# Encoder attention: statistics, a division of sums and scalings of a norm placed over three rounds of the second sequence of a pair instead of two

## The reference, cut to what matters

```python
q = (h @ wq + bq_); k = (h @ wk + bk_); v = (h @ wv + bv_)      # split into heads
scores = jnp.einsum('bhqd,bhkd->bhqk', q, k) * scale
scores = scores * smask
a = jax.nn.softmax(scores, axis=-1)
att = jnp.einsum('bhqk,bhkd->bhqd', a, v)
att = att.transpose(0, 2, 1, 3).reshape(Bx, Sx, Dx) @ wo + bo_
h = _ln(h + att, g1, be1)
ff = jax.nn.gelu(h @ w1 + b1_, approximate=False) @ w2 + b2_
h = _ln(h + ff, g2, be2)
```

## Time and profile before

| | |
|---|---|
| median of 3 runs | 4765.77 us (4759.86 to 4777.94) |
| the profiled execution | 4746.57 us, span 4744.7 us |
| PE busy | 3758.3 us, 79% of the span |
| PEld busy | 2577.3 us, 54% |
| DVE busy | 2783.0 us, 59% |
| ACT busy | 1913.5 us, 40% |
| POOL busy | 778.8 us, 16% |
| largest group of instructions | DVE, reductions L748: x1152, 749.8 us |

### The profile page before, as it was taken

The page is one execution under the profiler, slowest core; times in us unless marked ns, Lnnn a source line. Parts: engine busy times, 40 slices in busy tenths (PEclk is TensorE's granted clock), DMA queues, the critical chain, the costliest instruction groups (busy, mean ns, idle before and its releaser), DMA issues. The chain is left out here.

```text
span 4744.7 us, 71737 instructions
## 1 busy us (share of the span) xinstructions
PE 3758.3 (79%) x27543; PEld 2577.3 (54%) x27543; DVE 2783.0 (59%) x6776; ACT 1913.5 (40%) x2979; POOL 778.8 (16%) x1058
## 2 busy tenths in 40 slices
PE   5998998998989989969999644577745465997996
PEld 3666666666666667647777311255423332443664
DVE  5756747747747657552222477888679865112673
ACT  2554554545645545533333333322212112332443
POOL 2222222222222122130000000000000032002221
PEclk8999999999999999989999766599857666998997
DMA  5414424424325234200000000000000000001440
GB/s 135 114 38 110 113 52 98 100 51 116 80 64 118 63 83 114 63 35 6 1 1 1 14 0 0 0 1 1 1 5 0 4 0 25 0 0 47 99 98 24
DMA packets 156736, 222.56 MB, mean 47 GB/s; under 512 B 16158, under 2 KB 136350, under 8 KB 139422
## 3 DMA queue, kind: packets, MB, share of 16 engines
q10 hardware_dynamic: 19656, 107.37, 10.3%
q1 hardware_dynamic: 136750, 110.69, 8.6%
HBM read 154.42 MB, written 60.82 MB: 45 GB/s over the span
## 5 line engine op out<-in xcount | busy, mean ns | idle before, releaser
L748 DVE TENSOR_REDUCE enc_mx<-psum 128x2 f32<-128x512 f32 (+1 forms) x1152 | 749.8, 685 | 296.0 <-PE psum L457 292.6
L889 ACT ACTIVATE enc_e<-psum 128x1024 f32<-128x1024 f32 (+1 forms) x768 | 580.9, 808 | 423.5 <-PE psum L476 367.6
L457 PE MATMUL psum<-enc_ks,enc_qs 80*128 80x128 bf16 (+1 forms) x3072 | 459.4, 255 | 124.9 <-DVE enc_mx L748 108.9
L476 PE MATMUL psum<-enc_qs,enc_ks 83*128 83x256 bf16 (+1 forms) x3072 | 383.9, 250 | 20.4 <-DMA enc_qs<-enc_turned_max 15.5
L457 PEld LDWEIGHTS psum<-enc_ks,enc_qs 80*128 80x128 bf16 x3072 | 220.3, 100 | 264.8 <-DVE enc_mx L748 174.7
L487 PE MATMUL psum<-enc_e,enc_v 128*32 128x256 f32 (+1 forms) x6144 | 336.7, 338 | 0.0
L476 PEld LDWEIGHTS psum<-enc_qs,enc_ks 83*128 83x128 bf16 x3072 | 261.9, 99 | 58.2 <-DMA enc_qs<-enc_turned_max 20.1
L1764 ACT ACTIVATE moe_act_h<-psum 128x512 f32<-128x512 f32 x288 | 169.3, 598 | 306.0 <-PE psum L1638 305.8
L1660 PEld LDWEIGHTS psum<-par_s,moe_act_h 128*128 128x128 f32 x2304 | 269.7, 192 | 30.1 <-issue 28.5
L1727 DVE SCALAR_TENSOR_TENSOR moe_acc<-psum,moe_gates,moe_acc 128x128 f32<-128x128 f32 x256 | 72.1, 344 | 345.3 <-PE psum L1660 345.3
L1660 PE MATMUL psum<-par_s,moe_act_h 128*128 128x128 f32 x2304 | 272.6, 275 | 0.0
(11 more groups left out here) (457 smaller groups left out, 7380.3 us busy)
## 6 DMA issues: line engine op xcount, KB each, us to landing
enc_qs<-q_pieces ACTq DMA_DIRECT2D x234, 192.0 KB
enc_ks<-k_pieces ACTq DMA_DIRECT2D x234, 192.0 KB
k_pieces<-enc_pieces SPq DMA_DIRECT2D x240, 128.0 KB, 2.0
q_pieces<-enc_pieces SPq DMA_DIRECT2D x144, 128.0 KB, 2.0
enc_qs<-q_pieces SPq DMA_DIRECT2D x54, 192.0 KB
enc_ks<-k_pieces SPq DMA_DIRECT2D x54, 192.0 KB
rope_qs<-q_pieces ACTq DMA_DIRECT2D x39, 192.0 KB
rope_ks<-k_pieces ACTq DMA_DIRECT2D x39, 192.0 KB
```

What stands on the lines that cost most here:

```text
L457: last = T_.matmul(p1[f % 2][:, i * kw:(i + 1) * kw], qs[0:KEYED, slot, h, j * P:(j + 1) * P], ks[0:KEYED, slot, h, 0:kw], start=True, sto ...
L476: last = T_.matmul(p2[ch][:, g], ks[0:SCORED, slot, 4 * T + g, ch * P:(ch + 1) * P], qs[0:SCORED, slot, 4 * T + g, 0:n], start=True, stop= ...
L748: V.tensor_reduce(mx[:, u % 2, j * HEADS + h0:j * HEADS + h0 + n], p1[f % 2].rearrange("p (h k) -> p h k", h=n), AX_X, ALU.max)\
L889: A.activation(e_of(T, ch), p2[ch], ACT.Exp, scale=HD ** -0.5).then_inc(s_e, 1)
```

## The change

`Chain.statistics` is split in two: `gather` (the four `bn_stats`) and `combine` (the rest). In the attention loop of DVE the second sequence of a pair is ordered anew. `gather` stays in round 1. `combine` goes into round 2, between its first and second reduction. `normalise(layer, u - 1, 1)` goes from the end of round 1 into round 2, between its second and third reduction. The two halves of `apply` go from round 2 to the same places of round 3. In the first sequence of a pair, `normalise(layer, u - 1, 1)` stays where it was. No instruction is added or taken away, and no other engine's stream is touched.

```diff
     def statistics(self, dve, n):
+        self.gather(dve, n)
+        self.combine(dve, n)
+
+    def gather(self, dve, n):
         V = self.c.nc.vector
         dve.wait_ge(self.s_moved, n + 1)
         for t in range(TILES):
             last = V.bn_stats(self.stats[:, t, :], self.rows[:, t, :])
         last.then_inc(self.s_stats, 1)
+
+    def combine(self, dve, n):
+        V = self.c.nc.vector
         dve.wait_ge(self.s_stats, n + 1)
         V.memset(self.c.scratch[:], 0.0)
         for t in range(TILES):
...
                         red(0)
                         if T == 2 and odd and m:
+                            N1.combine(dve, at(layer, GROUPS, m - 1))
+                        if T == 3 and odd and m:
                             N1.apply(dve, at(layer, GROUPS, m - 1), (0, 1))
                         red(1)
-                        if T == 2 and odd and m:
+                        if T == 2 and odd:
+                            normalise(layer, u - 1, 1)
+                        if T == 3 and odd and m:
                             N1.apply(dve, at(layer, GROUPS, m - 1), (2, 3))
...
                         if T == 1 and odd and m:
-                            N1.statistics(dve, at(layer, GROUPS, m - 1))
-                        if T == 1 and u:
+                            N1.gather(dve, at(layer, GROUPS, m - 1))
+                        if T == 1 and u and not odd:
                             normalise(layer, u - 1, 1)
```

## The result

The changed kernel takes 4699.16 us, the median of 4 runs (4693.41 to 4704.41), beside 4770.71 us for the kernel before (4759.86 to 4777.94). The ratio is 0.9862, with a 95% interval of 0.9839 to 0.9885: 66 us less, between 55 and 77; the two medians by themselves lie 72 us apart. The forecast was faster, by 42 us. The rest of this document is about why the walk along DVE's work was right to a few hundredths of a microsecond, while the total was too small and the cause given for the falls of the clock was wrong.

A forecast was written before the change was run, and what follows sets the result against it. DVE was taken to set the pace in round 2 of full odd sequences, PE in the other rounds. A shorter DVE chain (21.6 us) plus the clock (20 us) gave 41.6 us: 4705 against the profile, 4724 against the median; range 4700 to 4754.

The forecast's parts named there:

- The walk through one odd sequence: Rounds 2 and 3 of full odd sequences: DVE's new order, timed with old distances, makes each sequence 0.60 us shorter.
- fill 10: PE's fill in round 2 behind the moved normalisation: it comes at 888.12, with a new wait of 0.8 us.
- The term of 0.60 us: Gain per full odd sequence from DVE's shorter chain up to the last scaling: 36 x 0.60 = 21.6 us.
- What is moved or passed at no cost: POOL's inverse root, bank reuse, exponentials, DMA and sequences 1 and 15: the reordering loses nothing there.
- The slow rival of blocked scalings: Round 3: GpSimd blocks the moved scalings, the last comes 2.7 us later, 76 us slower, 4842; chance 0.02.
- I take all of it: Slow clock in 12 of 36 third rounds, 1.66 us each: all 20 us counted as gain, bounds 0 to 20.
- the single wait of 1.18 us: PE's wait for a reduction in round 2 of odd sequences, taken to precede the clock's falls; it goes.
- The clock falls as often: Third rounds of odd sequences: waits shrink but as many are slow, 26 us gained, 4740; chance 0.15.
- no gain: DVE's chain to the last scaling: new handoffs eat the 0.60 us, leaving noise and some clock, 4760; chance 0.11.
- More than that: DVE's later work starts without pause and new waits overlap: 55 us gained with the clock, 4711; chance 0.06.
- the 69.8: PE's three waits for DVE, 1.94 us per odd sequence, over 36: 69.8 us, upper bound of the waits term.
- The spreading slow clock: Round 3 of odd sequences: later waits cause falls costing 2.6 us each, 52 us slower if all 36, 4818; chance 0.06.

The follow-up runs named there:

- e5: The changed kernel with four more `bn_stats`, into a tile nothing reads, ahead of `gather` in round 1 of odd sequences: 4759.17 us, ratio to the kernel before 0.9976.
- e6: The changed kernel with `gather` moved to round 0 of the odd sequence and `combine` to round 1: 4677.86 us, ratio to the kernel before 0.9803.
- e9: The changed kernel with `gather` and `combine` together again in round 1: a single run, 4715.42 us, beside 4763.15 us for the kernel before.
- e3: The kernel before, unedited, profiled again for its granted clock: 4772.29 us.
- e4: The kernel before, unedited, profiled once more after e3: 4770.91 us.
- e8: The changed kernel, unedited, run again on the chip of e5 to e7: 4708.77 us, ratio to the kernel before 0.9862.
- e1: The kernel before with only the scalings moved from round 2 to round 3 of odd sequences: 4713.13 us, ratio 0.9907.
- e2: The kernel before with only the normalisation moved from the end of round 1 to behind round 2's second reduction in odd sequences: 4825.03 us, ratio 1.0125.
- e7: As e6, with the normalisation back in round 1 and scalings split between rounds 2 and 3: 4650.66 us, ratio to the kernel before 0.9739.

## Why the prediction was right, and where it was off

- **The walk through one odd sequence** was right step by step. Forecast on the old scale: fill 10 at 888.12, the norm turned at 890.44. Measured, with 17.06 added: 888.08 and 890.40. Rounds 2.33 and 4.85, forecast "about 2.4" and "about 4.8". The term of 0.60 us measured 0.62, 22.3 us for the 36. e5, e6 and e9 change the chain by +0.78, -1.3 and +0.12 us and land within 0.06 us of the same walk.
- **What is moved or passed at no cost** held: POOL's root lies between 869.03 and 870.05, the scalings come at 871.48. Sequence 1 costs next to nothing: in layer 0 fill 10 waits 0.25 us, and PE's wait for the DMA at the start of sequence 2 falls from 0.63 to 0.32 us. The slow rival of blocked scalings falls: the four take 0.60 and 0.59 in pairs, as before. By the rule of the Trainium skill (SBUF — State Buffer, SBUF: two separate sides) they could only have been blocked beside a working GpSimd. In the third round POOL has only its root (1.02 us in the window that starts at 868.95), over before the scalings: the trace is in line with the rule, but no run here tests it.
- **The clock was the term that was mis-sized.** "I take all of it", 20 us, was read from one execution in which 12 of 36 third rounds were slow. That part did come out: 42.5 us in rounds 2 and 3 of the profiled pair (300.6 to 258.1), forecast 41.6. But two more executions had 20 and 22 slow rounds. Against the mean of the two profiles of the changed kernel, e3 and e4 lose 56 us in rounds 2 and 3 (313.2 and 316.4 to 258.3), 22 by the chain and 34 by the clock. A step was missing besides: the falls reach into the next even sequence's first round, which gave 5 us in the profiled pair and 8 in e3 and e4. By these two profiles the clock was worth 42 us and not 20, together 64 us with the chain, beside 66 by the ratio and 72 by the medians. That they meet so well is in part luck. e3 and e4 are as long as the median of the runs of the first result (4770.71 us), but 12 us or more above the median of seven runs of the same kernel on their own chip (4758.70 us). And their spans are 78 us longer than that of the changed kernel in its first profile, and 62 than in e8, with the same 64 us in these rounds. The profiled pair by itself gives 20 and 5 us for the clock; its 42.5 and 5.3 us leave 5 of the 53, which lie between the counted stretches of the layers and behind the encoder. The term lies between 25 and 42 us; how many rounds were slow in the timed runs wasn't seen.
- **The cause given for the falls was wrong.** The prediction tied them to the single wait of 1.18 us. e1 keeps that wait and shows no fall; e5 has no wait over 0.81 and shows 7 (e1, e2, e3 and e4 ran on one chip, so this isn't a difference between chips). What goes along with them, roughly, is PE's rest in the two rounds together:

| kernel | PE's rests in rounds 2 and 3 in most sequences, in order, us | sum | third rounds below 1.00, of 36 |
|---|---|---|---|
| e7 | 0.27 | 0.27 | 0 |
| e6 | 0.25, 0.35 | 0.60 | 0 |
| changed (two profiles) | 0.81, 0.35 | 1.16 | 0, 0 |
| e9 | 0.34, 0.74, 0.35 | 1.43 | 0 |
| e1 | 1.18, 0.41 | 1.59 | 0 |
| e5 | 0.49, 0.26, 0.81, 0.35 | 1.91 | 7 |
| before (three profiles) | 1.18, 0.27, 0.49 | 1.94 | 12, 20, 22 |
| e2 | 0.34, 0.91, 1.32 | 2.57 | 35 |

 The timelines also say where the clock falls: in none of the 54 slow rounds of the three profiles of before right behind the wait of 1.18 us. The first slow matmuls come behind the second rest or behind the third. These two of layer 0 and layer 5 are an example of each; a fill takes 0.61 us there instead of 0.40:

```profile
276.58 0.61 PE L457 MATMUL psum<-enc_ks,enc_qs 80*128 80x128 bf16 x4 [0.49 <-DVE enc_mx L748]
```

```profile
1901.37 0.61 PE L457 MATMUL psum<-enc_ks,enc_qs 80*128 80x128 bf16 x4 [0.28 <-DVE enc_mx L748]
```

 In e5 it is behind the third, after 1.56 us of rest. So the sum alone isn't the rule: e1 has 1.59 us of rest up to the turned norm and no fall. There PE works for 3.14 us without a rest between its two (215.28 to 218.42), in the kernel before for 0.84 us between the first and the second. How close the rests stand to each other seems to count too. Which of it sets off a fall, and why there are 7 in e5 and 12 to 22 in before, stays open.
- **The rivals.** "The clock falls as often" and "no gain" are out. "More than that" (55 us) came nearest in size, for a wrong reason: the chain gave 22 us and not half of the 69.8, and the clock more than its 20. The spreading slow clock is out for this change, but e2 shows it as a real thing, in 35 of 36 rounds.
- **The range** was 4700 to 4754; the ratio times the median shown at first gives 4700.0, the median itself is 4699.2, at its very edge. The three timed runs of the kernel before were all above the profiled one by 13 us or more; that gap was stated and not used. It was a sign that the clock term could be larger in the runs than in the profile. It is the clock term that puts the result at the edge.

## What to carry to other kernels

When two engines take turns within a round, count the work of the slower one from the last point where it rested to the point where the faster one needs it; that sum, not the place of the longest wait, said what a new order was worth in each of the kernels tried here, and the largest gain was in moving work ahead of that point, into a pause. Read a term that depends on the granted clock from several executions before it is put into a sum. And try the parts of a reordering alone: here one part made 44 us, another cost 60, and going further in the same direction (e7) made 58 more.

## What the runs showed of the hardware

- TensorE's clock fell to 1.2 GHz (granted clock 0.50 between 159.4 and 161.4 us of e5) with no rest longer than 0.81 us, and stayed at 2.4 behind one of about 1.18 us (e1). A slow third round costs 1.65 us on average, and the same kernel had 12, 20 and 22 of them in three executions: 13 and 16 of the 26 and 24 us between their spans.
- A wait of VectorE for its own earlier `bn_stats` costs 0.13 us, which another instruction in between hides (e9).
